# Graph attention over 8192 nodes: order of the first loads, of the statistics of x and of row 0's work

## What is computed

```python
h      = relu(layernorm(x))                      # x: 8192 x 256 f32
g      = inlayer2 @ W.T + b                      # inlayer2: 8192 x 256, W: 128 x 256
f1, f2 = g @ w1 + b1, g @ w2 + b2
logits = f1[:, None] + f2[None, :]
bias   = NEG_BIG * (1.0 - (adj > 0))             # adj: 8192 x 8192 int32
coefs  = softmax(leaky_relu(logits, 0.01) + bias, axis=-1)
out    = x + coefs @ h
```

## Time and profile before

| | before |
| --- | --- |
| median of 3 runs | 1506.81 us (1506.67 to 1507.01) |
| the profiled execution | 1505.09 us |
| its span, first to last instruction | 1503.3 us |
| mean granted TensorE clock | 0.981 |
| PE busy | 1427.8 us (95%) |
| DVE busy | 1304.9 us (87%) |
| ACT busy | 593.6 us (39%) |
| POOL busy | 266.6 us (18%) |
| moved by DMA | 302.36 MB, mean 201 GB/s |

### The profile page before, as it was taken

One profiled execution on the slowest core, in us unless ns is written; L12 is line 12 of the kernel. 1 busy time (PEld: TensorE's weight loads), 2 busy tenths in 40 slices (PEclk: granted clock), 3 DMA queues, 4 the chain that ended last, 5 costly groups with the idle time before them and its releaser, 6 DMA issues.

```text
span 1503.3 us, 33329 instructions
## 1 busy us (share of the span) xinstructions
PE 1427.8 (95%) x12585; PEld 1245.0 (83%) x12585; DVE 1304.9 (87%) x1471; ACT 593.6 (39%) x648; POOL 266.6 (18%) x223
## 2 busy tenths in 40 slices
PE   7346999999999999999999999999999999999998
PEld 6234888888888888888888888888888888888887
DVE  6869989898989888898989898989888898989894
ACT  0435343443444344444434343434444444434330
POOL 0347111110111111111111011111111111101111
PEclk9768999999999999999999999999999999999999
DMA  9972999999999999999999999999999999999950
GB/s 299 222 161 60 219 219 220 219 221 216 213 208 208 209 212 210 208 209 207 215 208 209 209 213 209 208 208 213 209 207 209 209 214 206 211 208 212 210 108 11
DMA packets 110164, 302.36 MB, mean 201 GB/s; under 512 B 11716, under 2 KB 44612, under 8 KB 110148
## 3 DMA queue, kind: packets, MB, share of 16 engines
q1 hardware_dynamic: 104016, 296.40, 92.1%
q10 hardware_dynamic: 6132, 5.77, 1.3%
HBM read 293.73 MB, written 8.39 MB: 201 GB/s over the span
## 4 chain that ended last, share of the span: by engine, by line
PE 89%; SPq 4%; DVE 3%; DMA 2%; ACT 1%; issue 0%; POOL 0%; POOLq 0%; ACTq 0%; DVEq 0%
PE acc L734 60%; PE acc L736 30%; SPq L259 3%; DMA adj_sb<-in_adj_dram 1%; DMA H<-in_x_dram 1%; DVE H L556 1%; ACT h_f L389 1%; DVE stats L502 1%; SPq L264 1%; DVE H L555 0%; DVE wgt L570 0%; POOL H L325 0%; DVE h_add L549 0%; DVE wT L459 0%; DVE wT L581 0%
## 5 line engine op out<-in xcount | busy, mean ns | idle before, releaser
L734 PE MATMUL acc<-H,wT 128*128 128x257 f16 x8192 | 1371.0, 275 | 55.6 <-POOL H L325 55.6
L736 PE MATMUL acc<-H,wT 128*128 128x257 f16 x4096 | 1116.4, 273 | 0.0
L734 PEld LDWEIGHTS acc<-H,wT 128*128 128x128 bf16 x8192 | 796.6, 97 | 172.7 <-issue 57.9
L581 DVE STREAM_TRANSPOSE wT<-wgt 128x1024 f32<-128x1024 f32 x512 | 633.9, 1238 | 144.2 <-PE acc L736 144.2
L371 ACT ACTIVATE mask<-adj_sb 128x1024 bf16<-128x1024 int32 x512 | 529.1, 1054 | 569.5 <-DVE wgt L570 449.3
L570 DVE SCALAR_TENSOR_TENSOR wgt<-b_word,c_word,mask 128x1024 f32<-128x1024 f32 x512 | 636.6, 1255 | 0.0
L736 PEld LDWEIGHTS acc<-H,wT 128*128 128x128 f16 x4096 | 405.4, 99 | 53.0
L332 POOL TENSOR_TENSOR x_res<-o_raw,x_res 128x256 f32<-128x256 f32 x64 | 68.1, 1064 | 1133.9 <-ACT o_raw L378 1102.0
L378 ACT ACTIVATE o_raw<-acc,r_den 128x256 f32<-128x256 f32 x64 | 30.4, 474 | 263.7 <-DVE r_den L600 263.7
L337 POOL TENSOR_TENSOR o_sb<-o_sb,x_res 128x256 f32<-128x256 f32 x64 | 83.6, 1307 | 5.3
L334 POOL TENSOR_SCALAR o_sb<-h_mean,no_nb 128x256 f32<-128x256 f32 x64 | 60.1, 939 | 0.0
(11 more groups left out here) (70 smaller groups left out, 95.9 us busy)
## 6 DMA issues: line engine op xcount, KB each, us to landing
adj_sb<-in_adj_dram SPq DMA_DIRECT2D x512, 512.0 KB, 8.9
x_res<-in_x_dram SPq DMA_DIRECT2D x64, 128.0 KB, 4.1
out_dram<-o_sb SPq DMA_DIRECT2D x64, 128.0 KB, 4.5
H<-in_x_dram SPq DMA_DIRECT2D x26, 256.0 KB, 12.8
wgt<-in_L_gnn_inlayer_dram ACTq DMA_DIRECT2D x8, 256.0 KB, 9.6
wgt<-in_L_gnn_inlayer_dram SPq DMA_DIRECT2D x8, 256.0 KB, 10.1
adj_sb<-in_L_gnn_inlayer_dram ACTq DMA_DIRECT2D x8, 256.0 KB, 12.6
adj_sb<-in_L_gnn_inlayer_dram SPq DMA_DIRECT2D x8, 256.0 KB, 13.0
```

Source lines behind the costliest of these rows:

```text
L581: nc.vector.transpose(wT[:, k % 4, :, :].rearrange("p t (g r) -> p g t r", g=Q), wgt[:, c, :, s * SQ:(s + 1) * SQ]).then_inc(t_ready, 1)
L734: pe.matmul(acc[:, par, 0:DV], w_hi[:, k % 4, t, :], H[:, j, part, 0:DV], start=(j == 0 and part == 0), stop=False)
L736: mm = pe.matmul(acc[:, par, 0:DV], w_lo[:, k % 4, t, :], H[:, j, 0, 0:DV], start=False, stop=(j == ROWS - 1))
```

## The change

The loads come in another order. All eight strips of inlayer2 and then all eight strips of x are issued first, on both queues (quadrants 0 and 1 on SP, 2 and 3 on ACT); adjacency follows on SP. In `load_adj` the four quadrants are issued as 0, 2, 1, 3. The statistics of x are taken by whole strips (`mean_var(k)` for eight tiles), those of strips 0 to 3 ahead of row 0, those of strips 4 to 7 in its first four strips. The first four mask parts of row 0 move behind the exponentials, between the first values. `pack_b(1)` moves behind the weights of chunk 0. The denominators are copied for a whole strip at a time. `affine` runs a strip further ahead. PE makes the exponents of chunk 0 after the last strip of inlayer2.

```diff
         def load_adj(eng, I, c):
-            for q in range(Q):
+            for q in (0, 2, 1, 3):
...
             for k in range(NS):
                 load_strip(eng, in2_stage(k), in2_q, k, in2_loaded[k], quadrants)
-                if k == SC - 1:
-                    load_strip(eng, x_stage(0), x_q, 0, xs_loaded[0], quadrants)
-            for k in range(1, 3):
+            for k in range(NS):
                 load_strip(eng, x_stage(k), x_q, k, xs_loaded[k], quadrants)
...
             load_adj(sp, 0, 0)
-            load_strip(sp, x_stage(3), x_q, 3, xs_loaded[3], range(Q))
             sp.wait_ge(in2T_ready, 2 * 8)
             load_adj(sp, 0, 1)
-            for k in range(4, NS):
-                load_strip(sp, x_stage(k), x_q, k, xs_loaded[k], range(Q))
...
-            rstds(0)
-            rstds(1)
+            for k in range(4):
+                rstds(k)
             for k in range(NS):
                 low_of_values(2 * k)
-                if k + 2 < NS:
-                    rstds(k + 2)
+                if 1 <= k <= 4:
+                    rstds(k + 3)
                 low_of_values(2 * k + 1)
...
-            for g in range(Q):
-                mask_part(0, g, 0)
...
+            mask_part(0, 0, 0)
+            mask_part(0, 1, 0)
             values(0)
+            mask_part(0, 2, 0)
+            mask_part(0, 3, 0)
             values(1)
-            act.wait_ge(packed, 1)
-            mask_part(0, 0, 1)
...
-                for m in ((5, 6), (7, 8), (9,), (10, 11), (12,), (13,), (14,), (15,))[u]:
+                if u == 0:
+                    act.wait_ge(packed, 1)
+                for m in ((4,), (5, 6), (7, 8), (9,), (10, 11), (12, 13), (14,), (15,))[u]:
...
-            for k in range(2, NS):
-                if k == 7:
-                    chunk_f(0)
+            for k in range(2, 6):
                 turn_in2(k)
-                if 4 <= k < 7:
-                    raw_stats(3 * (k - 4), 3 * (k - 3))
-            raw_stats(9, 16)
-            for n in range(4):
-                mean_var(n)
-            raw_stats(16, 20)
+            raw_stats(0, 4)
+            turn_in2(6)
+            raw_stats(4, 8)
+            turn_in2(7)
+            mean_var(0)
+            raw_stats(8, 16)
+            mean_var(1)
+            chunk_f(0)
+            raw_stats(16, 24)
             chunk_f(1)
+            raw_stats(24, 25)
...
             weights(0, 0, 0)
-            affine(1)
+            mean_var(3)
+            weights(0, 1, 0)
             high_of_values(0)
-            weights(0, 1, 0)
-            half_stats(5)
+            weights(0, 2, 0)
             high_of_values(1)
-            weights(0, 2, 0)
             weights(0, 3, 0)
+            pack_b(1).then_inc(packed, 1)
+            affine(2)
...
-                        if u + 3 < NS:
-                            half_stats(2 * u + 6)
+                        if u < 4:
+                            raw_stats(TS * (u + 4), TS * (u + 4) + HALF)
                         if u + 1 < NS:
                             high_of_values(2 * u + 3)
-                        if u + 2 < NS:
-                            affine(u + 2)
+                        if u < 4:
+                            raw_stats(TS * (u + 4) + HALF, TS * (u + 5))
                         if u + 3 < NS:
-                            half_stats(2 * u + 7)
+                            affine(u + 3)
+                        if u < 4:
+                            mean_var(u + 4)
```

More of the change, by code:

```diff
@@ L502, in raw_stats, with mean_var @@
                     nc.vector.bn_stats(out=stats[:, j, :], in_=x_stage(j // TS)[:, j % TS, :]).then_inc(stats_ready, 1)
-            def mean_var(n):
-                at = slice(HALF * n, HALF * (n + 1))
-                dve.wait_ge(stats_ready, HALF * (n + 1))
-                for j in range(HALF * n, HALF * (n + 1)):
+            def mean_var(k):
+                at = slice(TS * k, TS * (k + 1))
+                dve.wait_ge(stats_ready, TS * (k + 1))
+                for j in range(TS * k, TS * (k + 1)):
                     ins = nc.vector.bn_aggr(out=mv[:, j, :], in_=stats[:, j, :])
@@ L533, in _ @@
             then_wait(nc.vector.tensor_tensor(tiny[:, 4:5], cst[:, 0:1], cst[:, 1:2], ALU.add))
+            raw_stats(25, 26)
             dve.wait_ge(F_ps_ready, 1)
@@ L554, in high_of_values @@
                 dve.wait_ge(h_ready, HALF * (n + 1))
-                nc.vector.tensor_copy(H[:, at, :, D], D_parts[:, at, :])
+                if n % 2 == 1:
+                    nc.vector.tensor_copy(H[:, HALF * (n - 1):HALF * (n + 1), :, D],
+                                          D_parts[:, HALF * (n - 1):HALF * (n + 1), :])
                 nc.vector.tensor_copy(H[:, at, 0, 0:D], h_f32[:, n % HR, :, :]).then_inc(hi_ready, 1)
@@ L600, in finish_2 @@
                 nc.vector.reciprocal(r_den[:, par:par + 1], den[:, par:par + 1]).then_inc(fin_step, 1)
+            mean_var(2)
+            raw_stats(26, 32)
             dve.wait_ge(D_exp, 2)
@@ L605, in _ @@
             affine(0)
-            mean_var(4)
             then_wait(pack_b(0))
+            affine(1)
             dve.wait_ge(c_exp, 1)
             then_wait(pack(c_word[:, :], c_f32[:, :]))
-            pack_b(1).then_inc(packed, 1)
             nc.vector.tensor_copy(D_parts[:, :, 0], D_big[:, :])
@@ L710, in _ @@
             for k in range(NS):
-                if k == 6:
-                    pe.wait_ge(f2_of_ready, 1)
-                    b_exponents(0)
                 f_of_strip(k)
+            pe.wait_ge(f2_of_ready, 1)
+            b_exponents(0)
             b_exponents(1)
```

5 lines of the change are left out of this document (1 added, 4 removed).

## The result

| | before | after |
|---|---|---|
| median of the runs | 1506.74 us (4 runs, 1505.00 to 1507.01) | 1492.20 us (4 runs, 1492.05 to 1493.02) |
| profiled execution, its span | 1505.1, 1503.3 us | 1492.2, 1490.4 us |
| first mask of row 0 | 51.78 us | 66.01 us |
| first product of row 0 | 74.27 us | 81.50 us |
| row 1 begins | 157.47 us | 144.58 us |

The changed kernel is faster: the ratio of the times is 0.9909, with a 95% interval of 0.9897 to 0.9921. That is 14.5 us by the medians and 12.9 us by the spans of the two profiled executions. All of the gain lies ahead of row 1, whose start moved by 12.9 us, as much as the span.

The account below looks back on a forecast made before the run. Products on PE bound the kernel from row 1 on, so its start at 157.47 us sets the end. First product +7.2, hole -13.8, row 0 +0.3 give -6.3 us: 1500.5 us, range 1495.5 to 1503.5.

Parts of the forecast that it names:

- The loads: Before row 0: inlayer2 and x at 349 GB/s until 54.3 us, adjacency at 217; first masks at 66.8 us, 15 later.
- The hole: In row 0, ACT waits 14.62 us for row tile 1's adjacency and DVE stands 13.80 us; its removal gives -13.8 us.
- The prologue: Before the first mask, ACT's issues and DVE's added statistics lie under the adjacency wait: cost zero, almost 5 us of cover.
- The first product: Row 0's first product comes at 81.5 us, +7.2 us against 74.27, between 80.6 and 82.6 by one POOL collision.
- From row 1 on: From row 1 to the end, the same 1345.8 us as before.
- The quadrants: Adjacency loads in the order 0, 2, 1, 3: 217 GB/s taken; 349 kept as a rival, 1496.8 us, chance 0.18.
- The lower bound: For adjacency loads, alternating the halves of the partitions gains nothing and the rate stays 217 GB/s.
- the step "Row 0": Row 0's strips take 69.7 us together, against 69.4 before without ACT's wait for row tile 1: +0.3 us.
- The ring: In row 0's strips 0 to 3, a loop of waits through DVE, POOL and ACT sets 10.5 us, against 9.9 before.
- The collision with POOL: In row 0, DVE's cast takes 2.62 instead of 0.68 us once POOL's subtraction has begun; one more or less is 2 us.

Follow-up runs that it names:

- the loads alone: Kernel before, with only the load order changed (inlayer2 and x on both queues, then adjacency on SP; quadrants as before): 1508.95 us, ratio 1.0020.
- the subtraction cut short: Kernel before and changed kernel, each with POOL's low part of the values computed for 32 of 256 columns only: 1484.17 and 1468.88 us.
- kernel with the old order: Changed kernel with the first four strips of row 0 ordered as before, statistics aggregated in two halves of four: 1496.24 us, ratio 0.9935.
- Loads and masks: Kernel before with the changed load order and row 0's four chunk 0 masks moved behind the exponentials on ACT: 1498.94 us, ratio 0.9951.
- the six statistics: Changed kernel with six statistics instead of four behind the first cast in the first four strips of row 0: 1492.90 us, ratio 0.9916.

## Why the prediction was wrong

**Right.** *The loads*: two queues kept their rate to about 53 us (360 GB/s from 40 to 53, 349 forecast to 54.3), and the first mask came at 66.01 us, 66.8 forecast; 1.2 us of the changed kernel's is the alternation, so without it the sum was 0.4 us too early. *The hole* went, by the way that was named: row tile 1 is issued from 71.90 us, and its masks don't wait. *The prologue* cost nothing: DVE was idle for 6.05 us, almost 5 forecast. *The first product*: 81.50 us, 81.5 forecast. That it fits to the digit is luck: the figure holds half a collision of the second cast with POOL, 1 us; what came was a whole one of another instruction, the packing at 2.65 instead of 0.75 us, and the first mask was 0.8 us early. The experiment with the loads alone shows that the masks' place behind the exponentials belongs to this step: without it the product comes at 89.67 us. *From row 1 on*: the same, 1345.8 us.

**The quadrants.** The lower bound was taken because the second and third transfer of a lone chunk lie 2.6 us apart. The order 0, 2, 1, 3 gives 6% (215 to 229 GB/s), 1.2 us. The Trainium skill (SBUF — State Buffer, "Can I just issue two DMAs to hit both halves?") says that a transfer at partition 0 and a concurrent one at partition 64 moved only 6% more than a single one, and that two can't be fused to reach all ports. The 6% measured here for neighbours on one queue agree with that. The two queues do not: with one on each half 349 GB/s were moved, with SP alone 217, and row 0's adjacency came at 296 instead of 226 GB/s when both issued it. There the measurement decides; no run separates the second queue from the other half.

**Wrong: the step "Row 0", +0.3 us, in truth -6.3.** Its 6.6 us are all by which the difference of the spans, 12.9, exceeds the forecast of 6.3. The rest of the medians' 14.5 us, 1.6, is that the profiled execution of the kernel before lies below its median and that of the changed kernel at it. Strips 0 to 3 took 36.8 us and not 43.8, the last four 26.3 and not 25.9. Behind it stands a second term of wrong size: the hole's removal was put at -13.8 us and is worth 11.9, as the kernel with the loads alone shows, since the hole had also spared one cast its wait behind POOL. Row 0 without the hole is 71.3 us and not 69.4, and against that the strips gave 8.2 us. Three things in the step failed.

1. *The ring was not the bound.* Its members were each read off the trace of before, and its sum of 10.5 us was longer than what that trace showed, 9.9 us a strip with DVE busy for 98% of it. That should have been the warning: a ring of 10.5 us can't run in 9.9. Nor was rstd newly ahead of a low part: in both kernels POOL's code has it between the two low parts of a strip. In the rows of the changed kernel the ring closes after two strips (88.45 to 105.46 us), so its sum of 10.5 us would ask for 5.3 us a strip and no more. ACT's values do wait for POOL's low part (14.7 us in five waits), but they are ready 2.4 to 3.7 us ahead of DVE's casts, and no instruction of DVE waits for them in strips 1 to 3. With the subtraction cut short, both kernels run at DVE's own work, 7.8 and 7.2 us.
2. *Its parts were too large for the new order.* Eight aggregations in a row and the addition take 0.74 us from 96.04 us to the next start at 96.78, and not 0.9; against the two halves of before that is 0.33 us, and 0.22 more are saved because no aggregation stands right behind its statistics. The forecast had moving the statistics down as no gain in these strips.
3. *The collision with POOL* was carried over at its old price. In the kernel before, the small copy gets in ahead of POOL's second subtraction and the cast behind it stands for the whole of it, 2.62 us. In the changed one a copy and an affine meet the ends of the two subtractions, 0.6 us each: 1.27 a strip in place of 2.03. The kernel with the old order has both sides, though with the halves as well: 9.76 us a strip with the cast at 2.63 us, 8.50 without, and 0.70 of the 1.26 between them by the waits.

**What was settled, in us of span.** Three steps lead from one kernel to the other. Loads and masks: -5.6. From there to the changed kernel with the old strip: -3.7, in which are strip 4 without statistics (-3.0), strips 5 and 6 (-1.2, cause open), the alternating quadrants (-1.2, measured by themselves) and about +2 ahead of the first product, for which the packing that now meets POOL is the likely cause. The order inside the strip with the aggregations in one row: -3.6. In all -12.9. The loads alone are worth +3.5, so they can't be priced by themselves. The prediction had the first step, and a strip fewer with statistics (though at the ring's price for the others); the third it left out. That loads and masks alone bring row 1 to 151.86 us, close to the forecast 151.2, is in part luck as well: their first product comes 0.9 us before the forecast's, and row 0 takes 71.25 us and not 69.7.

**What stays open.** Why POOL's pair is at times entered by a waiting instruction of DVE and at times not was read from rows after the event: two edits, the cast ahead of the copy and the six statistics, moved the wait to another instruction, which then took 2.11 and 1.78 us. A rule from which the place of the wait can be computed ahead was not found.

## What to carry to other kernels

When a chain of waits is put together from single rows, hold its sum against the pitch that the trace shows: if it is longer than what the kernel already runs at, one of its links is not a link or it closes only after more than one round, and the engine that is busy for 98% of the stretch is the bound. A load moved earlier pays only if no instruction that others need stands in front of the one that waits for it; here the same order of loads was worth +3.5 or -5.6 us by where four masks stood. And an idle stretch ahead of the first product is a place to fill: work moved there filled 2.8 us of it, and the time fell by 3.0.

## What was new about the chip

**Who gets in between DVE and POOL.** POOL's subtraction reads two tensors from SBUF. The Trainium skill (SBUF — State Buffer, "Who interferes with whom") says that such work and certain instructions of DVE share a pair of ports, and that whoever comes first keeps it for the whole instruction. The rows agree: copies of 8 or 16 elements take 2.11 and 0.81 us in place of 0.19, a cast 2.63 in place of 0.68. What the rows add is the order when both have work queued. POOL's pair of subtractions takes 4.87 us when a copy and a cast of DVE get in between them, and 4.35 when only the copy does; the cast behind the copy then stands for the whole second subtraction. That the small copy uses up the turn is how these rows read; no edit tested it by itself.

**A small move with an effect on PE.** In the two kernels in which the second product of a pair reads the high part again, PE's steady part is faster too, though it was no part of the edit. The stretch from 200 to 1400 us (PE's busy time and its products), of the kernel before, and then of the kernel before with the short subtraction:

```profile
200.00:1400.00 1200.00, 1200.00 (x10836) 1.00 0.99 211
```

```profile
200.00:1400.00 1200.00, 1200.00 (x10911) 1.00 0.99 212
```

That is 110.7 against 110.0 ns a product at the same clock, and 9 us from row 1 to the end (1336.6 us in both kernels with the short subtraction, 1345.8 in the others); that is the part of those two spans that row 0 does not explain. Whether it is the repeated operand or something else was not tried.
